# A two-layer graph network on one core: in the stage that builds the node table, the gathers of edge sources are issued in one run and ten of thirteen feature scalings move from GpSimd to the vector engine

## The reference

```python
h = jnp.maximum(_layernorm(x, axis=-1), 0.0)
# layer 1: linear, batch norm over the nodes, then a normalized graph sum
H = h @ W.T + b
H = (H - mu) * rsqrt(var + BN_EPS) * gamma + beta
deg_hat = 1.0 + segment_sum(ones, dst); dinv = rsqrt(deg_hat)
out = segment_sum(H[src] * (dinv[src] * dinv[dst])[:, None], dst)
x = x + relu(out + H * (dinv * dinv)[:, None])
# layer 2: the edge attributes summed by destination, then an MLP of three layers
h = jnp.maximum(_layernorm(x, axis=-1), 0.0)
agg = segment_sum(edge_attr, dst)
x = x + mlp(concat([h, agg, u[batch]]))
```

## Time and profile before

| | |
|---|---|
| median of 3 runs | 767.58 us (767.42 to 768.07) |
| profiled execution, first to last instruction | 766.9 us |
| median of the runs less that span | 0.7 us |
| busy, share of the span | PE 90%, DVE 75%, ACT 59%, POOL 18% |
| table stage, first DVE instruction to the last | 78.8 to 135.7 us |
| edge loop, first matmul | 139.4 us |
| moved by DMA | 119.75 MB |

### The profile page before, as it was taken

One profiled execution on the slowest core, in us unless ns is written; L12 is line 12 of the kernel. 1 busy time (PEld: TensorE's weight loads), 2 busy tenths in 40 slices (PEclk: granted clock), 3 DMA queues, 4 the chain that ended last, 5 costly groups with the idle time before them and its releaser, 6 DMA issues. The chain is left out here.

```text
span 766.9 us, 21741 instructions
## 1 busy us (share of the span) xinstructions
PE 688.6 (90%) x9010; PEld 585.7 (76%) x9010; DVE 576.1 (75%) x1133; ACT 451.6 (59%) x795; POOL 141.4 (18%) x182
## 2 busy tenths in 40 slices
PE   0898644589999999999999999999999999998996
PEld 0766534478888888888888888988888888886554
DVE  5998862798878888788877877668888887845632
ACT  1443544376666666666666666556666666666862
POOL 3502780111111111111110011101000000003532
PEclk9998685599999999999999999999999999999999
DMA  6300610265545555555544444455555555461122
GB/s 163 94 1 1 241 46 2 71 230 183 185 173 195 205 206 205 206 205 205 182 174 171 172 171 172 191 208 207 207 207 208 206 206 205 171 174 29 28 68 72
DMA packets 64877, 119.75 MB, mean 156 GB/s; under 512 B 3077, under 2 KB 22739, under 8 KB 64807
## 3 DMA queue, kind: packets, MB, share of 16 engines
q1 hardware_dynamic: 64246, 117.89, 43.8%
q0 software_dynamic: 576, 1.12, 0.6%
HBM read 115.81 MB, written 4.03 MB: 156 GB/s over the span
## 5 line engine op out<-in xcount | busy, mean ns | idle before, releaser
L1514 PE MATMUL ps_product<-counts_sb,table_sb 128*128 128x240 f16 (+1 forms) x2646 | 416.7, 261 | 0.0
L1504 PE MATMUL ps_counts<-key_hot,lo_hot 128*128 128x147 bf16 x2096 | 389.1, 231 | 16.2 <-ACT counts_sb L1335 9.5
L1335 ACT CAST counts_sb<-ps_counts 128x588 f16<-128x588 f32 x524 | 336.2, 650 | 112.7 <-PE ps_counts L1504 67.1
L1504 PEld LDWEIGHTS ps_counts<-key_hot,lo_hot 128*128 128x128 bf16 x2096 | 199.3, 98 | 65.0 <-issue 26.6
L1514 PEld LDWEIGHTS ps_product<-counts_sb,table_sb 128*128 128x128 f16 x2646 | 240.2, 97 | 8.0
L1384 DVE TENSOR_TENSOR key_hot<-key,iota_key 128x1176 bf16<-128x1176 f16 x262 | 200.5, 765 | 0.0
L1379 DVE TENSOR_TENSOR lo_hot<-src_lo,iota_key 128x1024 bf16<-128x1024 f16 x262 | 180.9, 691 | 23.8 <-PE ps_counts L1504 20.6
L1319 POOL TENSOR_SCALAR place_hot<-iota_c,slot_now 128x96 f32<-128x96 f32 x81 | 60.5, 759 | 491.1 <-PE ps_place L1540 469.0
L1395 DVE TENSOR_TENSOR attr_hot<-rel,iota_w 128x640 f32<-128x640 int16 x81 | 66.9, 826 | 59.3 <-PE ps_sums L1528 59.3
L1528 PE MATMUL ps_sums<-attr,attr_hot 128*32 128x128 f32 x3240 | 96.0, 277 | 0.0
L1528 PEld LDWEIGHTS ps_sums<-attr,attr_hot 128*32 128x32 f32 x3240 | 88.6, 111 | 5.4 <-issue 4.9
(11 more groups left out here) (276 smaller groups left out, 550.7 us busy)
## 6 DMA issues: line engine op xcount, KB each, us to landing
attr<-in_edge_attr_dram SPq DMA_DIRECT2D x80, 1280.0 KB, 7.5
acc<-in_x_dram SPq DMA_DIRECT2D x4, 768.0 KB, 8.4
attr<-in_x_dram SPq DMA_DIRECT2D x12, 256.0 KB, 5.1
out_dram<-y_ring SPq DMA_DIRECT2D x12, 256.0 KB, 2.3
src_padded<-in_src_dram SPq DMA_DIRECT2D x1, 805.7 KB, 7.5
attr<-in_edge_attr_dram SPq DMA_DIRECT2D x2, 320.0 KB, 8.1
attr<-in_edge_attr_dram SPq DMA_DIRECT2D x1, 640.0 KB, 3.9
raw_d<-in_dst_dram SPq DMA_DIRECT2D x1, 540.0 KB
```

Of the source, the lines that this page charges most:

```text
L1335: act.copy(counts_sb[s % 2][:].rearrange("p h (n t) -> p h n t", n=WN) [:, :, :, k * QUAD:(k + 1) * QUAD], ps_counts[n % 2][:, :, 0:KEYS]. ...
L1504: ins = pe.matmul(ps_counts[quad % 2][:, c, 0:KEYS], lo_hot[:, held, pair, :, q % 2], key_hot[:, held, pair, :, q % 2], start=True, stop=True)
L1514: ins = pe.matmul(ps_product[side][:, 0:SLOTS] if tiles == TS else product, table_sb[:, h, low, :], counts_sb[side][:, h, :] if tiles == T ...
```

## The change

- POOL scales chunks 0, 1 and 2 alone (`SCALED_AHEAD = 3`), then issues all 17 gathers and the spare gather one behind the other.
- DVE scales chunks 3 to 12: two ahead of its loop, then chunk `c + 5` behind `save_low_part(c)`. It counts on a semaphore of its own, `scaled_late`, on which PE's `turn_rows` waits from chunk 3 on.
- DVE: the marks come after chunks 1, 2 and 4 (before: 1, 4, 6); `split_sources` 0 and 1 after chunks 5 and 8 (before: 8 and 10), the others behind the last chunk as before; counting and choosing of spares after 6 (5), bounding after 9 (7), bases after 11 (10).
- PE: `turn_keys` 0 and 1 in turns 7 and 10 (before 10 and 12); the matmuls for `before` in turn 5 (4), `sum_spares` in 8 (7), `turn_bases` in 11 (9).
- ACT: `save_low` 0 and 1 in turns 6 and 9 (9 and 11), `save_keys` 0 and 1 in 8 and 11 (11 and 13).

```diff
+            SCALED_AHEAD = 3
...
+            def scale(engine, c):
+                n = width(c) * P
+                engine.tensor_scalar(scaled[:, c, 0:n], h_t[:, c * NC:c * NC + n], bn[:, 4:5], bn[:, 6:7],
+                                     ALU.mult, ALU.add).then_inc(scaled_ok if c < SCALED_AHEAD else scaled_late, 1)
...
                     pool.wait_ge(affine, 1)
-                    for c in range(CHUNKS):
-                        scale(c)
-                        if c >= 5:
-                            gather_sources(c - 5)
-                    for k in range(CHUNKS - 5, MC):
+                    for c in range(SCALED_AHEAD):
+                        scale(pool, c)
+                    for k in range(MC):
                         gather_sources(k)
                     gather_spares(pool, spares_bounded, spare_in)
...
                     def turn_rows(c):
-                        pe.wait_ge(scaled_ok, c + 1)
+                        if c < SCALED_AHEAD:
+                            pe.wait_ge(scaled_ok, c + 1)
+                        else:
+                            pe.wait_ge(scaled_late, c + 1 - SCALED_AHEAD)
...
                         if c == 7:
+                            turn_keys(0)
+                        if c == 8:
                             sum_spares(pe, plan_spare, spare_hot[:], spares_chosen, spares_summed)
-                        if c == 9:
+                        if c == 10:
+                            turn_keys(1)
+                        if c == 11:
                             turn_bases(pe, plan_base, spares_bounded, spares_based)
...
+                    for c in range(SCALED_AHEAD, SCALED_AHEAD + 2):
+                        scale(v, c)
                     for c in range(CHUNKS):
                         save_low_part(c)
+                        if c + SCALED_AHEAD + 2 < CHUNKS:
+                            scale(v, c + SCALED_AHEAD + 2)
...
                         if c == 5:
+                            split_sources(0)
+                        if c == 6:
                             count_spares()
                             choose_spares(v, link, spare_shift[:], spare_hot[:], spares_chosen)
-                        if c == 6:
-                            mark(2).then_inc(marked, 1)
-                        if c == 7:
+                        if c == 8:
+                            split_sources(1)
+                        if c == 9:
                             bound_spares(v, link, plan_spare, spares_summed, spares_bounded)
```

More of the change, by code:

```diff
@@ L879, in _ @@
                 def _(pool):
-                    def scale(c):
-                        n = width(c) * P
-                        pool.tensor_scalar(scaled[:, c, 0:n], h_t[:, c * NC:c * NC + n], bn[:, 4:5], bn[:, 6:7],
-                                           ALU.mult, ALU.add).then_inc(scaled_ok, 1)
                     def gather_sources(k):
@@ L958, in _ @@
                             pe.matmul(plan_column, over_16[:, 0:GC], ones_16[:], start=True, stop=True).then_inc(column_ready, 1)
-                        if c == 4:
+                        if c == 5:
                             pe.wait_ge(column_saved, 1)
@@ L1012, in _ @@
                             save_high(c)
-                        if c == 9:
+                        if c == 6:
                             save_low(0)
-                        if c == 11:
-                            save_low(1)
                         if c >= 2:
                             save_self(c - 2)
+                        if c == 8:
+                            save_keys(0)
+                        if c == 9:
+                            save_low(1)
                         if c == 11:
-                            save_keys(0)
-                        if c == 13:
                             save_keys(1)
@@ L1108, in _ @@
                             v.tensor_copy(of_column[:], plan_column).then_inc(column_saved, 1)
+                        if c == 2:
+                            mark(1)
                         if c == 4:
-                            mark(1)
+                            mark(2).then_inc(marked, 1)
                         if c == 5:
+                            split_sources(0)
+                        if c == 6:
                             count_spares()
                             choose_spares(v, link, spare_shift[:], spare_hot[:], spares_chosen)
-                        if c == 6:
-                            mark(2).then_inc(marked, 1)
-                        if c == 7:
+                        if c == 8:
+                            split_sources(1)
+                        if c == 9:
                             bound_spares(v, link, plan_spare, spares_summed, spares_bounded)
-                        if c == 8:
-                            split_sources(0)
-                        if c == 10:
+                        if c == 11:
                             save_bases(v, plan_base, spares_based)
-                            split_sources(1)
-                    for b in range(2, KEY_BATCHES):
+                        if c == 12:
+                            split_sources(2)
+                    for b in range(3, KEY_BATCHES):
                         split_sources(b)
```

8 lines of the change are left out of this document (2 added, 6 removed).

## The result

The changed kernel takes 764.24 us in the median of 4 runs (762.84 to 764.94), the kernel before beside it 767.5; the ratio is 0.9945, 95% interval 0.993 to 0.996. That is faster by 3 us, a third of the 9.6 us that I forecast. The profiled execution took 764.53 us with a span of 762.8. In the table, the length of the table stage is counted as in the table ahead of the prediction, from DVE's first instruction to its last.

What follows compares the result with a forecast made beforehand. DVE was taken to bound the table stage up to about 108, then a stall of PE's completions. Stage end 126.0 against 135.7 gave -9.7 us, span 757.2, plus 0.7 to the median: 758 us, range 754.5 to 773.5.

Steps and rivals of the forecast that it cites:

- the stall: Table stage before: ACT and DVE stand some 8.1 us, released at 117.2, though PE's awaited matmuls are recorded as done.
- Scales at 0.52 us: Ten scales added to DVE in the table stage: 0.52 us each, 0.46 after overlap, 4.4 us in all.
- The slow instructions beside POOL's scales: DVE operations on SBUF slowed beside POOL's scales (0.90 against 0.44 us); removal gives about 0.8 us before 85.48, 0.9 behind.
- Splits at 99 and 106: DVE's early source splits: `split_sources(0)` forecast at about 99; the first two key turns wait for splits at about 100 and 107.
- The waits of DVE without a stall: DVE's chunk loop returning to a PSUM bank after three chunks: 1.7 us of waits before, taken as 2.0.
- From the end of `split_sources(2)` to the end 10.1 us: Tail of the table stage: `save_low(2)` 0.64 us, then 9.45 us from key batch 2's start on PE; end at 126.0.
- By its own merit worth little: Without its 8.1 us stall the old order would end near 127.6 too; most of the 9.7 us gain is the stall.
- the two facts for the gathers: POOL tie: late completion of 105.12 soon after gathers follow without scales at 102.53; release 2.4 us after the last gather.
- the case without a stall: Rival: table stage ends at 126.0, kernel at 758 us, own range 754.5 to 761; chance 0.48.
- D: Rival: unbroken gathers cause the stall, from about 86 to 107.1; stage ends at 142.0, 773.5 us; chance 0.25.
- C: Rival: the stall returns once with its old 8.1 us, between chunk 4 and key batch 2; 766.5 us; chance 0.17.
- B: Rival: DVE's scales fight the gathers, about 1.0 us each instead of 0.46, 5.4 us more; 763 us; chance 0.10.

Runs made afterwards that it cites:

- e6: Kernel before, with a memset of 700 columns ahead of each of its nine tail gathers (1.8 us apart); 759.14 us, ratio 0.9882.
- e12: Changed kernel with gathers 9 to 16 each waiting for a semaphore of DVE's or ACT's work, no memsets; 758.66 us, ratio 0.9866.
- e2: Changed kernel with a 0.6 us memset on POOL behind gathers 8 to 16, to stand some 1.75 us apart; 758.67 us, ratio 0.9891.
- e1: Changed kernel without the 17 indirect gathers, five plain loads on SP's queue instead (output of wrong edges); 755.29 us, ratio 0.9841.
- e5: Changed kernel with a memset of 300 columns behind gathers 7 to 15, pitch 1.48 to 1.71 us; 759.06 us, ratio 0.9884.
- e13: Changed kernel with fewer PE matmuls: one a block in turn_self instead of two, three a column in turn_keys instead of five; 762.12 us, ratio 0.9916.
- e3: Changed kernel with marks, splits, key batches and spare steps placed as in the kernel before; 762.16 us, ratio 0.9925.
- e8: Changed kernel with a memset of 700 columns behind every one of gathers 0 to 15, pitch 1.8 us throughout; 762.32 us, ratio 0.9915.
- e7b: Changed kernel whose gathers fetch 32 instead of 128 sources per row, the rest of src_raw zeros; 766.03 us, ratio 0.9962.
- e14: Changed kernel with gathers 8 to 16 replaced by plain DMAs of the same size from fixed addresses; 755.00 us, ratio 0.9822.
- e11: Changed kernel with three memsets of 2000 columns, behind gathers 7, 10 and 13, so gathers come in runs of three; 764.79 us, ratio 0.995.

## Why the prediction was wrong

**The step that failed** is the one on which all was said to depend: "if the stall does not come back". It came back, 5.90 us of DVE. Of the stage's length the parts are now measured. Without a stall the old order takes 47.5 us (e6) and the new one 46.5 (e12). So the stall cost 9.3 us before and costs 4.8 now, while the unbroken run of gathers ends 4.7 us earlier, and the change by its own merit gives 1.1: together the 5.6 us by which the stage became shorter. With e2 (45.8) in place of e12 the stall costs 5.5 now and the change by itself gives some 1.7; the clock of the tail can move these by 0.6.

**The rest of the working held.** Scales at 0.52 us, 4.4 in all: they are 0.53 us. The slow instructions beside POOL's scales: L193 0.44 us where it was 0.90. (That row is an instruction with two tensors from SBUF, and I set it beside a rule told of `tensor_scalar`; the row of that kind is the one of 17 columns, 0.54 us before and 0.17 now.) Splits at 99 and 106. The waits of DVE without a stall, which I took at 2.0 us, are 0.5 (e1) to 2.1 us (e5, e12). From the end of `split_sources(2)` to the end 10.1 us: e2 shows 10.1. The forecast for no stall was 758; the changed kernel without a stall takes 758.7 to 759.1. "By its own merit worth little" is what e6 measured.

**Where the judgement went wrong** is the weighing of the evidence on the cause. I had the two facts for the gathers: the first late completion soon after they stood close, and the release 2.4 us after the last. I set against them that the gathers from 85.1 on did nothing. But in the kernel before these stood between scales of POOL, 2.0 to 3.1 us apart; in e2 already 1.8 is nearly harmless. They were no evidence, and I had named the alternation myself in "when gathers first follow without a scale between". That gave the case without a stall 0.48. I also took the completion of 105.12 for the first late one; `sum_spares` at 99.63 was 1.0 us late already, which is only seen in its semaphore, as no engine stood waiting for it.

**The rivals.** D had the cause right and its place wrong. It put the beginning at 86; the first five gathers of the changed kernel do start 1.25 to 1.5 us apart there, and one completion is 0.7 us late (recorded at 89.72, read at 90.48), but no more. Two things are different in that stretch, and no run separates them: the attribute loads fill the DMA engines (1.03 of their time), and PE has 24 matmuls from 85 to 90, 58 from 100 to 105. Gathers 4, 5 and 7, counted from 0, were then stretched to 1.96 to 2.58 us, and the free run of eight begins at 100.4. So its size was that of C: C's 766.5 (its own sum gives 766.0) is 2 us above what was measured, for the stall was shorter than before. I had priced C with the old length although its end would move with the last gather; 8.1 less those 4.7 would have given 3.4, and 5.9 was measured. B fell: the scales took 0.53 to 0.64 us beside the gathers, not 1.0. That its 763 lies nearest to the measured 764.24 is chance. And that the time fell by more than some 1 us, the change's own merit, rests on the stall having become shorter, which no rival had.

## What to carry to other kernels

When a wait ends with nothing recorded that could release it, find out what it goes with before moving work around it: one kernel with the suspect left out (e1) and one with it spaced (e2) cost less than a reordering, and would have shown that 8.9 us (768.01 to 759.14) were to be had in the old order with one line. Where such a wait goes with close indirect gathers, try them further apart (1.5 us was enough here) while TensorE has work that others wait for, and pace them by semaphores of work that is there anyway rather than by memory operations on GpSimd. And when a case is excluded because "it didn't happen earlier", check first that the earlier stretch had the same conditions.

## What the runs showed of the hardware

- Indirect gathers by GpSimd at a pitch of 1.25 us, each of 128 rows, hold back what TensorE's readers see: by 3.1 and 9.4 us in the kernel before, 5.3 in the changed one, 7.1 in e13, but by 1.3 us in e3. After an unbroken run of eight or more the long delays end 1.5 to 2.4 us behind the last gather. At a pitch of 1.5 us completions are late by up to 1.8 and 1.9 us (e5, e12); at 1.8 us by 0.7 in e2, by 1.4 in e8; at 2.0 us and more still once by 0.9 to 1.0, at `sum_spares` (before, e6). A quarter of the bytes changes nothing (e7b), and nine plain DMAs 0.55 us apart do nothing (e14). By which path the gathers reach TensorE stays open: its supply of instructions, its execution or its completions may be what is slowed, and no run tells these apart. Every time on record comes with a span and a clock from a profile, so no run excludes either that the taking of the records has a part in it. The Trainium skill (SBUF — State Buffer, Who interferes with whom) says of the engines' access to SBUF that PE never waits on anyone; if that holds here, this wait comes another way, which no run tests.
- The same section of the Trainium skill says that a DVE `tensor_scalar` in a two-port mode and GpSimd block each other for a whole instruction, and counts the writing of descriptors with that. For memsets the trace agrees: a scale of 0.53 us took up to 1.61 in e8, and 1.92 in e11 beside a memset of 1.79. For the indirect gathers it does not: scales took 0.53 to 0.61 us while they were issued (e5, e12), and 0.64 at most in the changed kernel.
- In a close run of gathers single ones cost POOL 1.96 to 2.59 us in place of 0.95. Full DMA engines do not explain all of it: in the changed kernel those at 89.21 and 91.47 fell in the time of the loads (1.03 and 0.99 of the DMA engines' time), the one of 2.58 us at 95.65 did not (0.14 to 0.16); and in e8, with the same loads and a pitch of 1.8 us, none took over 1.24 us.
